# A fused AdaLN and FFN kernel with mixtures of LoRA experts: inputs laid out with columns on partitions, routers joined to A and Wb

## What is computed

```python
# layer 0, cond: logits + 5 for the batch's language, top 2, softmax
logits = einsum('btd,ed->bte', x, Wr) + bias
h = einsum('btd,erd->bter', x, A)
c = einsum('btd,od->bto', x, W) + 2 * einsum('bter,bte,eor->bto', h, gates, B)
# layer 0, ffn: top 1, the route's own weight
wh = route_weight[..., None] * einsum('bsd,erd->bser', c, A)
x = x + einsum('bser,eor->bso', wh, Bw)
# layer 1, cond: one adapter per batch
c = x @ W.T + b + 2 * (x @ lora_As[m]) @ lora_Bs[m]
# layer 1, ffn: base plus top-2 LoRA
x = x + c @ W_base.T + b_base + 2 * einsum('ter,te,eor->to', h(c), w(c), B)
```

## Time and profile before

| what | value |
|---|---|
| median of 3 runs | 478.28 us (477.41 to 480.46) |
| span of the profiled execution | 478.9 us |
| TensorE busy | 464.3 us, 97% |
| VectorE busy | 326.1 us, 68% |
| ScalarE busy | 154.5 us, 32% |
| GpSimd busy | 72.4 us, 15% |
| moved by DMA | 40.25 MB in 88689 packets, 68647 of them under 512 B |
| TensorE's mean granted clock | 0.996 of full |

### The profile page before, as it was taken

One profiled execution on the slowest core, in us unless ns is written; L12 is line 12 of the kernel. 1 busy time (PEld: TensorE's weight loads), 2 busy tenths in 40 slices (PEclk: granted clock), 3 DMA queues, 4 the chain that ended last, 5 costly groups with the idle time before them and its releaser, 6 DMA issues.

```text
span 478.9 us, 8348 instructions
## 1 busy us (share of the span) xinstructions
PE 464.3 (97%) x2911; PEld 430.5 (90%) x2911; DVE 326.1 (68%) x956; ACT 154.5 (32%) x340; POOL 72.4 (15%) x64
## 2 busy tenths in 40 slices
PE   5899999999999999999999999999999999999997
PEld 4898899999999898988999999999999999999986
DVE  2757956576575797849848857856865974973852
ACT  3646620232312265223224313323423323421310
POOL 2021000000000242130230240240221222220110
PEclk9899999999999999999999999999999999999999
DMA  8994348511111201321421420440241242110202
GB/s 243 391 307 168 92 130 171 149 44 45 44 45 44 50 6 21 47 45 62 96 46 59 98 46 17 114 70 16 96 73 14 106 62 35 62 51 2 103 3 88
DMA packets 88689, 40.25 MB, mean 84 GB/s; under 512 B 68647, under 2 KB 82737, under 8 KB 88526
## 3 DMA queue, kind: packets, MB, share of 16 engines
q1 hardware_dynamic: 88558, 39.81, 32.1%
q0 software_dynamic: 96, 0.00, 0.3%
HBM read 28.64 MB, written 11.16 MB: 83 GB/s over the span
## 4 chain that ended last, share of the span: by engine, by line
PE 87%; DVE 8%; DMA 2%; ACT 1%; issue 1%; SPq 0%; DVEq 0%; ACTq 0%
PE banks L1412 26%; PE banks L1414 26%; PE banks L1413 25%; PE banks L1422 3%; PE banks L1407 2%; DMA wraw<-in_L_cond_W_dram 2%; PE banks L1684 2%; DVE G L929 2%; PE banks L1483 1%; DVE left L929 1%; DVE ws_lo L929 1%; ACT left L668 1%; PE banks L1592 0%; DVE WbTlo L929 0%; DVE G_raw L1239 0%
## 5 line engine op out<-in xcount | busy, mean ns | idle before, releaser
L1412 PE MATMUL banks<-G,left 128*128 128x460 f32 x224 | 88.0, 393 | 0.0
L1413 PE MATMUL banks<-G,left 128*128 128x460 f32 x224 | 82.9, 370 | 0.0
L1414 PE MATMUL banks<-G,left 128*128 128x460 f32 x224 | 82.9, 370 | 0.0
L1412 PE MATMUL banks<-WbThi,ws_hi 128*128 128x460 f32 (+1 forms) x216 | 75.1, 348 | 0.7 <-DVE ws_lo L929 0.7
L608 POOL TENSOR_TENSOR xTlo<-x_raw,xThi 128x512 fp32r<-128x512 f32 x28 | 37.9, 1375 | 248.4 <-ACT xThi L668 116.7
L1414 PE MATMUL banks<-WbThi,ws_lo 128*128 128x460 f32 (+1 forms) x216 | 73.3, 340 | 0.0
L1413 PE MATMUL banks<-WbTlo,ws_hi 128*128 128x460 f32 (+1 forms) x216 | 73.1, 338 | 0.0
L668 ACT ACTIVATE left<-x_raw 128x512 fp32r<-128x512 f32 x64 | 38.8, 629 | 60.0 <-DVE x_raw L1092 29.3
L1412 PEld LDWEIGHTS banks<-G,left 128*128 128x128 f32 x224 | 42.4, 189 | 4.5 <-DVE wzTlo L929 0.3
L1414 PEld LDWEIGHTS banks<-G,left 128*128 128x128 f32 x224 | 42.0, 188 | 4.7
L1413 PEld LDWEIGHTS banks<-G,left 128*128 128x128 f32 x224 | 42.3, 189 | 2.6
(11 more groups left out here) (213 smaller groups left out, 1003.0 us busy)
## 6 DMA issues: line engine op xcount, KB each, us to landing
x_raw<-in_x_dram SPq DMA_DIRECT2D x56, 128.0 KB, 3.7
out_dram<-ybuf SPq DMA_DIRECT2D x14, 512.0 KB, 2.7
x_raw<-in_L_cond_W_dram SPq DMA_DIRECT2D x10, 512.0 KB, 6.7
wraw<-in_L_cond_W_dram SPq DMA_DIRECT2D x5, 512.0 KB, 8.8
wraw<-in_L_ffn_W_base_dram SPq DMA_DIRECT2D x4, 512.0 KB, 9.4
x_raw<-in_L_ffn_W_base_dram SPq DMA_DIRECT2D x4, 512.0 KB, 8.0
a0f<-in_L_ffn_A_dram SPq DMA_DIRECT2D x2, 512.0 KB, 8.8
xin_first<-in_x_dram SPq DMA_DIRECT2D x1, 1024.0 KB, 13.7
```

The source lines that it names most:

```text
L1412: pe.matmul(out_, l[0], r[0], start=start, stop=False, **kw)
L1413: pe.matmul(out_, l[0], r[1], start=False, stop=False, **kw)
L1414: return pe.matmul(out_, l[1], r[0], start=False, stop=stop, **kw)
```

## The change

The host's part of the file (`kernel`) reshapes, transposes and joins the inputs in numpy, and the program receives them as it wants them in SBUF: every weight has its inner columns on partitions. R0 is `route_w` joined to A of layer 0's ffn; A0 is A of the cond joined to its router; F0, F1 and F2 are the three column chunks of the joined router, A and Wb of layer 1 (F1 and F2 come in two halves, so there are five parts: F0, F1a, F1b, F2a, F2b). x comes as `xT`, batch by batch, and `lora_As` and `lora_Bs` come turned per adapter.

```diff
+    def by_c(t):
+        return t.reshape(t.shape[0], K, P).transpose(2, 1, 0)
+    ffn1 = by_c(_np.concatenate([W_router, A1.reshape(ER, D), Wb]))
+    f0, f1, f2 = (ffn1[:, :, c0:c0 + n] for c0, n in CHUNKS)
+    laid = dict(
+        xT=x.reshape(NB, TPB, P, K, P).transpose(0, 4, 1, 3, 2).reshape(NB, P, TPB * D),
+        R0=by_c(_np.concatenate([route_w, A0f.reshape(ER, D)])),
+        A0=by_c(_np.concatenate([A0c.reshape(ER, D), Wr0])),
```

On the chip all transposes of inputs go: `turn_units`, `turn_x` on both engines, the turn of `brow`, and the scratch passes through `x1T_dram` and `b1_dram`. What is left of a unit is a copy on ScalarE and a remainder on VectorE, now from SBUF and over whole parts. The raw values land in the bytes in which the remainder will stand, and the remainder is taken in place:

```diff
+        def twin(name, shape, where=None):
+            with ExitStack() as landing:
+                raw = sb(f"{name}_raw", shape, where=landing)
+            return sb(name, shape, F32R, where), raw
...
+            def f_split(i):
+                lo_in(f_hi, i + 1, f_part(i, 1), f_part(i, 2), f_part(i, 0), f_lo)
```

W1 now lands in one buffer, `w1raw` (half of `x_raw1`), so a row's load waits for the split of the row before it:

```diff
+            for s in range(2, K):
+                sp.wait_ge(w1_hi, s)
+                sp.wait_ge(w1_lo, s)
+                load_w1(s)
```

Batch 0's delta is added to its raw x by one VectorE instruction a quarter (`x1_add`) in place of two. The split of B1 moves from the end of M into slot 0, where `lora(0)` waits for it. `ffn0` stands after M's row 0 instead of inside it, and tile 1's `add_lora0` and gate transposes stand inside row 0. In TensorE's program the start reads:

```diff
+            pe.wait_ge(bs_lo, 1)
+            pe.wait_ge(f_lo, 1)
+            fe_steps(0, K)
+            pe.wait_ge(a0_lo, 1)
+            pe.wait_ge(c0_lo, 2)
+            pe.wait_ge(d0w_lo, 1)
+            small0(0, first_tile(0), 1)
+            pe.wait_ge(f_lo, 2)
+            fe_steps(K, 12)
+            pe.wait_ge(f_lo, 3)
+            fe_steps(12, 2 * K)
+            pe.wait_ge(ident_ready, 1)
+            turn_small(hg_ready, 1, pt_hg, hg[:, :], thg_done)
+            pe.wait_ge(f_lo, 4)
+            fe_steps(2 * K, 18)
+            add_lora0(0)
+            fe_steps(18, 20)
+            pe.wait_ge(f_lo, 5)
+            fe_steps(20, 22)
+            turn_small(wh_ready, 1, pt_wh, wh[:, :], twh_done)
+            small0(1, first_tile(1), 2)
+            fe_steps(22, 3 * K)
```

More of the change, by code:

```diff
@@ L12, with adaln_ffn @@
 ACT = mybir.ActivationFunctionType
[L24 to L33, removed]
-    C0C = ER + E + RC
[L35 to L42, removed]
+NB, TPB, K, E, R, D = 8, 2, 8, 8, 16, 1024
+ER = E * R
+RC = E + ER
+MC = RC + D
+ZC = R + RC
+DW = 256
+SW = (R + MC - DW) // 2
+KH = K // 2
+Y_OF = [(0, DW - ZC), (DW - ZC, SW), (DW - ZC + SW, SW)]
+CHUNKS = [(0, DW - R), (DW - R, SW), (DW - R + SW, SW)]
+def adaln_ffn(nc, xT, lang_ids, slot_ids, W0, R0, A0, B0, Bw, W1, b1, lora_As, lora_Bs, F0, F1, F2, b_base, B1, out):
+    C0C = ER + E + RC
     LANG_BIAS = 5.0
-    GROUPS = [(0, 3), (3, 3), (6, 2)]
-    assert (NB, K, E, R, TPB, ER) == (8, 8, 8, 16, 2, 128)
-    xf = x.rearrange("b s d -> (b s) d")
     outf = out.rearrange("b s d -> (b s) d")
@@ L102, in adaln_ffn @@
         with ExitStack() as first:
[L104 to L115, removed]
+            R0T, R0raw = twin("R0T", [P, K, 2 * RC], first)
+            R0Thi, R0Tlo, R0raw = R0T[:, :, 0:RC], R0T[:, :, RC:2 * RC], R0raw[:, :, RC:2 * RC]
+            b0hi, (b0lo, b0raw) = sb("b0hi", [P, D], F32R, first), twin("b0lo", [P, D], first)
+            w0s_hi, w0s = list(ws_hi), list(ws)
+            for i in range(2, K):
+                w0s_hi.append(sb(f"w0s_hi{i}", [P, D], F32R, first))
+                w0s.append(twin(f"w0s_lo{i}", [P, D], first))
+            w0s_lo, w0raw = [t for t, _ in w0s], [raw for _, raw in w0s]
+            hsum = [sb(f"c0_sum{i}", [P, 4 * RC], where=first) for i in range(2)]
+        xT_first = [w0s_hi[2:4], w0s_lo[2:4]]
+        w1raw = x_raw1[:, D:2 * D]
         G, G_raw = [], []
@@ L134, in adaln_ffn @@
         right_factors(1)
[L136 to L140, removed]
         with ExitStack() as second:
@@ L144, in adaln_ffn @@
             for c in (1, 2, 0):
-                Wb_of[c] = [sb(f"WbT{n}{c}", [P, K, CHUNKS[c][1]], F32R, second) for n in ("hi", "lo")]
-        B1Thi, B1Tlo = ws_hi[0], ws_lo[0]
+                Wb_of[c] = [sb(f"WbThi{c}", [P, K, CHUNKS[c][1]], F32R, second),
+                            *twin(f"WbTlo{c}", [P, K, CHUNKS[c][1]], second)]
+        B1Thi, (B1Tlo, B1raw) = ws_hi[0], ws[0]
         right_factors(2)
@@ L436, in _ @@
-            sp.wait_ge(unit_done, 3)
-            sp.dma_start(a0f[:, :], A1.rearrange("e r d -> (e r) d")).then_inc(a1_in, 16)
-            sp.dma_start(routers[:, 1, :], W_router).then_inc(r1_in, 16)
+                load(w0raw[0][:, half], W0[0:P, half], w0_in[0] if h else w0_half_in)
+            load(w0raw[1][:, :], W0[P:2 * P, :], w0_in[1])
+            load_r0(1)
+            for j in range(2, K):
+                load(w0raw[j][:, :], W0[j * P:(j + 1) * P, :], w0_in[j])
+            load(b0raw[:, :], B0, b0_in)
```

649 lines of the change are left out of this document (239 added, 410 removed).

## The result

The changed kernel takes 467.18 us (median of 4 runs, 466.59 to 468.83) against 478.36 before: a ratio of 0.9766 (95% interval 0.9738 to 0.9794), 11.2 us less. The forecast was 465.0 within 460.5 to 472. This is time on the device; what numpy now does on the host ahead of it is not in it. The profiled execution of after took 466.59 us with a span of 464.7; every execution of the two kernels whose span and time are both known took 1.8 to 2.3 us longer than its span.

What follows compares the result with a forecast made beforehand. TensorE was taken to bound M and slots, its transposes to lengthen the start, where VectorE would then set the pace. Start -12.6, M -0.4, slot waits -0.9 and -0.4, B1 +0.2: -14.1 from 478.9, 464.8, said as 465.0 (460.5 to 472).

Steps and rivals of the forecast that it cites:

- one slow stretch: In the start, behind a TensorE wait: 14 products 0.226 us apart instead of 0.126, adding 1.4 us.
- the remainders in place: Remainders whose raw and result share bytes: the prediction fails if one costs clearly more than its row; no size given.
- hand-overs: In the start, a dozen hand-overs between engines at 0.1 us each move M's start from 54.4 to 55.6 us.
- B1's transposes: In M, eight transposes gone from TensorE save 0.8 us; half was credited, -0.4 us.
- wait of 1.2 us for hg ahead of slot 0: Between M and slot 0, VectorE loses two x transposes and two B1 splits, shortening TensorE's wait: -0.9 us.
- B: Rival: loads bound the start, lora_Bs or F late; F0 and all after slips 3 to 5 us, 469 us; chance 0.20.
- C: Rival: the clock stays low in two or three more stretches of the start, 469 to 471 us; chance 0.14.
- the rule that speaks against the change: In the start, activity releases TensorE's slow clock; removing early transposes and adding waits risks slow stretches, 1.4 us each.
- D: Rival: TensorE bounds the start with all feeds in time, M at 48 to 50 us, time 457 us; chance 0.05.
- E: Rival: in M, W1's single landing buffer stops TensorE each row; about 485 us at 13 us landings; chance 0.03.
- F: Rival: the change does nothing, VectorE already set the start, span within 1%; chance 0.03.
- VectorE as the engine that sets the start: From 27 to 49 us VectorE's remainders set the start, over 90% busy, with TensorE waiting on them.

Runs made afterwards that it cites:

- the second profile of before: The unchanged kernel before, profiled once more: 478.65 us (one run), span 476.5 us, mean clock 1.000.
- waits filled: Changed kernel plus 16 and 20 identity transposes on TensorE in two waits of the start, results unread: 465.51 us, ratio 0.9738.
- its second profile: The changed kernel run and profiled again without any edit: 467.55 us, ratio 0.977, span 466.5 us.

## Why the prediction was right, and where it was off

The direction and the place were right: the whole gain is in the start, by transposes gone from TensorE and c0, and the slots did not move. The terms of the sum, beside the profile of after (the forecast's share for M and for what follows it are told apart by the second profile of before: 107.73 less 0.4, and the rest):

| step | forecast, us | measured, us |
|---|---|---|
| first c0 product | 6.7 | 6.48 |
| c0's end | 27.0 | 25.48 |
| VectorE begins the first c0 sum | 27.2 | 24.45 |
| remainders of A0 and x together | 2.5 | 4.18 |
| D0's remainder done | 33.6 | 33.05 |
| hg of tile 0 done | 41.1 | 40.94 |
| last F part done | 48.8 | 48.75 |
| TensorE's longest wait | 2.5 | 2.43 |
| M starts, without the slow stretch | 55.6 | 54.77 (waits filled) |
| one slow stretch | 1.4 | 1.5 (7.26 less 5.72) |
| M starts | 57.0 | 56.07 |
| M | 107.3 | 108.06 |
| from M's end on | 300.5 | 300.57 |
| span | 464.8 | 464.7 |

The span came within 0.1 us, and that is partly luck: M's start came 0.9 us earlier than forecast and what follows it took 0.8 longer, 464.7 is the shortest of the eight known spans, and two more errors lie between the span and the time.

**The early start was better than forecast, and GpSimd's reads took it back.** W0's second block was copied at 7.48, not 10.6, so c0 never waited for it and ended 1.5 us earlier; `lora_Bs` was on ScalarE at 20.46, not 23. VectorE was 2.7 us ahead at the first c0 sum. It lost 0.85 us to ScalarE's copy of F0 and 1.7 to GpSimd, which the forecast had no term for. The forecast named the remainders in place as the price that no row of before could exclude; that was the wrong suspect, as the run with the c0 remainders on VectorE shows. From 33 us on the chain of VectorE and TensorE ran as worked out; its hand-overs came to 0.7 us where 1.2 was taken (without the slow stretch 21.5 us from D0's remainder to M, 20.8 by the forecast's steps alone).

**M gained nothing.** The forecast took 0.4 us off for B1's transposes. They are gone (0.8), but a wait of 0.46 for a remainder (`Mdir`) came at 139.36, so that M's last two rows are only 0.2 shorter, and row 0 takes 16.14 us instead of 15.63, since tile 1's add_lora0 and hg's transpose now stand in it. M is 0.3 longer. That the two had moved into M was known with the change; the sum left them out. The wait of 1.2 us for hg ahead of slot 0 and the one of 0.4 in slot 0 are gone, as forecast; a wait of 0.5 for `hs` is new.

**The base was wrong by two pieces.** The forecast took 14.1 us from the span of the profiled execution, 478.9, called it 0.6 above the median, and read the result as a time. The time of after is 1.8 to 1.9 us longer than its span, so 464.7 of span is 466.6 of time. And the profile of before had a stretch of slow clock behind the 1.99 us wait that the second profile doesn't have, and the clocks of the 21 other executions give no sign of it: c0's end there was 2.5 us later than in the second profile. So of the 14.1 us, 2.4 were there only against that one execution. From the second profile of before to that of after the gain is 476.5 to 464.7, 11.8, and by the medians 11.2. That the profiled execution's time is its span, as stood ahead of the forecast, holds for no execution whose time and span are both known.

**The rivals.** *B* happened only when it was forced, and then cost 8.7 us instead of the 3 to 5 of the forecast, since d0 and the narrow fold steps behind that wait ran slow as well. *C* happened in part: every run of the changed kernel has a mean clock of 0.993 to 0.996 where the kernel before, but for the profile of the forecast, has 0.999 to 1.000, and its second profile has two stretches, one more than the sum had. So the rule that speaks against the change was right, at 1.3 to 3 us of the gain; not where it was expected, since c0's slow start is free, but behind the waits that the change put into the start. *D* is refuted by four waits of 5.9 us in all. *E* did not come: the waits on `ws_lo` in M are none. *F* is out by the interval.

**The signs named in advance.** c0 at 6 to 7 us and done at 27 to 29: the first yes, the second earlier. Two or three waits for `WbTlo`, the longest 2 to 3 us and last: yes, three, 2.43. VectorE over 90% busy from 27 to 49: 19.27 of 22 us, 88%. M at 55 to 59: yes. The description of VectorE as the engine that sets the start was too simple in one point: moving small0 in TensorE's order gained 2.3 us of M's start with VectorE's work as it was. For work added to TensorE it held: 48 transposes cost 1.15 to 1.5 us by the medians.

## What to carry to other kernels

Before a trace serves as the base of a sum, compare its mean granted clock and its span with those of the other runs, and find out what lies between span and time: here these two were worth 4 us, the chain of 40 us itself was right to 1 us. When work moves from PSUM to SBUF operands, look at what GpSimd does at that moment, since two engines that did not touch each other before may now take turns. Where TensorE must wait for a remainder, put independent products that are ready ahead of the wait: it saves the wait and the slow clock behind it.

## What the runs showed of the hardware

- A wait of TensorE of 2.0 to 2.4 us may or may not be followed by slow products: behind the same 2.06 us wait one execution ran at 0.126 us a product and another at 0.23 for 13 products. Filled with transposes, no stretch came.
- In the first microseconds the record of the granted clock reads 1.00 while the products of c0 stand 0.226 us apart. Where equal products stand 0.226 us apart later on, the record reads 0.50 (51.00 to 53.40). So in the start the spacing tells the clock, the record does not.
- VectorE's and GpSimd's operations that both read SBUF slowed each other: 1.28 to 1.82 and 1.22 to 2.36 us on VectorE (1088 and 1024 columns, both inputs in SBUF), 1.36 and 1.34 to 2.79 and 2.18 on GpSimd (544 columns). Each ended 1.1 to 1.2 us after the other engine's operation that had begun before it.
- Eight gathers of 64 KB, each with its load of an index, held SyncE for 8.06 to 8.34 us wherever they stood.
